# Local attention: exponentials that read the scores from PSUM with the negated row maximum as bias

## What is computed

```python
def local_attention(q, k, v):          # windows of 64, keys of this window and the one before
    sim = jnp.einsum('bhwid,bhwjd->bhwij', bq, bk)
    sim = jnp.where(mask, -jnp.finfo(sim.dtype).max, sim)
    attn = jax.nn.softmax(sim, axis=-1)
    return jnp.einsum('bhwij,bhwjd->bhwid', attn, bv)
...
q = l2norm(q) * qs; k = l2norm(k) * ksc
q, k = rotary_xpos(q, k)
o = local_attention(q, k, v)
x = x + o @ wo
# then shift_token, layernorm, h @ w1 + b1, a * gelu(g), h @ w2 + b2, added to x
```

## Time and profile before

| what | value |
|---|---|
| median of three runs | 1563.13 us |
| the profiled execution | 1563.58 us |
| its span | 1561.7 us |
| PE busy | 1346.8 us, 86% of the span |
| DVE busy | 1145.6 us, 73% |
| ACT busy | 801.7 us, 51% |
| POOL busy | 724.0 us, 46% |
| granted TensorE clock, mean | 0.947 |

### The profile page before, as it was taken

The page is one execution under the profiler, slowest core; times in us unless marked ns, Lnnn a source line. Parts: engine busy times, 40 slices in busy tenths (PEclk is TensorE's granted clock), DMA queues, the critical chain, the costliest instruction groups (busy, mean ns, idle before and its releaser), DMA issues.

```text
span 1561.7 us, 39029 instructions
## 1 busy us (share of the span) xinstructions
PE 1346.8 (86%) x15968; PEld 970.4 (62%) x15968; DVE 1145.6 (73%) x2484; ACT 801.7 (51%) x1633; POOL 724.0 (46%) x562
## 2 busy tenths in 40 slices
PE   4545999988999999984999999967989999998797
PEld 3434878875777777762666666654556666665554
DVE  3776776434888888874888888864578888888565
ACT  1222223224666666653777777742457777776421
POOL 1752545541344433434666666632246666666100
PEclk7776999996999999997999999999999999999999
DMA  4000544500000000003000100011100000000011
GB/s 133 0 0 16 112 93 110 108 13 2 3 3 3 4 3 3 3 3 91 8 8 7 22 8 8 1 30 28 25 24 8 9 17 13 9 5 2 12 31 54
DMA packets 61837, 40.34 MB, mean 26 GB/s; under 512 B 41312, under 2 KB 51808, under 8 KB 61664
## 3 DMA queue, kind: packets, MB, share of 16 engines
q1 hardware_dynamic: 61664, 37.88, 10.2%
HBM read 27.12 MB, written 2.36 MB: 19 GB/s over the span
## 4 chain that ended last, share of the span: by engine, by line
PE 33%; ACT 8%; SPq 6%; DVE 4%; POOL 2%; issue 1%; DMA 1%; DVEq 0%; POOLq 0%; ACTq 0%
PE PS L1872 7%; SPq L1463 5%; PE PS L1923 5%; PE PS L1957 4%; PE PS L1914 4%; PE PS L1891 3%; PE PS L1937 2%; ACT e_oT L1787 2%; PE PS L1948 2%; ACT qk L1756 2%; ACT e_pm L1793 2%; PE PS L1907 2%; POOL rot L1537 2%; PE PS L2010 1%; PE PS L2019 1%
## 5 line engine op out<-in xcount | busy, mean ns | idle before, releaser
L1537 POOL TENSOR_TENSOR rot<-qk,sinl 128x1024 f32<-128x1024 f32 x64 | 217.6, 3401 | 139.4 <-DVE qk L1631 139.4
L1530 POOL TENSOR_TENSOR rn<-ss,neghalf 128x16 f32<-128x16 f32 x64 | 185.6, 2901 | 108.6 <-DVE ss L1624 108.6
L1756 ACT ACTIVATE qk<-PS 128x512 f32<-128x512 f32 x128 | 76.4, 597 | 135.7 <-PE PS L1872 135.7
L1102 DVE TENSOR_REDUCE d_mx<-PS 128x4 f32<-128x576 f32 x128 | 96.9, 757 | 66.3 <-PE PS L1246 63.3
L1872 PE MATMUL PS<-wqkv,hT 128*128 128x512 f32 x256 | 128.8, 626 | 10.9 <-DMA qks<-in_e_ks 5.7
L607 POOL TENSOR_TENSOR uu<-uu,cb 128x512 f32<-128x512 f32 x64 | 82.8, 1295 | 90.0 <-DVE uu L839 88.2
L1923 PE MATMUL PS<-ident,e_pm 128*128 128x128 f32 x512 | 84.5, 289 | 45.9 <-ACT e_pm L1793 44.3
L1923 PEld LDWEIGHTS PS<-ident,e_pm 128*128 128x128 f32 x512 | 55.9, 144 | 102.4 <-ACT e_pm L1793 95.7
L739 ACT ACTIVATE sg<-PS 128x512 f32<-128x512 f32 x72 | 43.0, 597 | 134.1 <-PE PS L667 133.0
L1165 ACT ACTIVATE pa<-PS 128x512 f32<-128x512 f32 x128 | 76.5, 597 | 61.8 <-PE PS L1255 61.7
L1610 DVE TENSOR_REDUCE e_mx<-PS 128x8 f32<-128x1024 f32 x64 | 78.2, 1222 | 30.7 <-PE PS L1914 30.6
(11 more groups left out here) (241 smaller groups left out, 3535.9 us busy)
## 6 DMA issues: line engine op xcount, KB each, us to landing
cb<-comb_rows SPq DMA_DIRECT2D x32, 512.0 KB, 9.1
X<-in_L_attn_x SPq DMA_DIRECT2D x4, 512.0 KB, 7.4
zs<-Z SPq DMA_DIRECT2D x64, 32.0 KB
zg<-Z SPq DMA_DIRECT2D x16, 128.0 KB
out_x<-X SPq DMA_DIRECT2D x8, 256.0 KB, 2.5
zs<-Z SPq DMA_DIRECT2D x64, 31.8 KB
zg<-Z SPq DMA_DIRECT2D x16, 127.0 KB
wqkv<-in_e_wqkv SPq DMA_DIRECT2D x2, 768.0 KB, 4.2
```

The source lines that it names most:

```text
L1102: chain(dve.tensor_reduce(mx[:, par, :, :], s, AX.X, ALU.max))
L1530: pool.tensor_tensor(rn[:, v % 2, :], ss[:, v % 2, :], c.neghalf[:, :], ALU.pow).then_inc(rn_ready.sem, 1)
L1537: pool.tensor_tensor(rot[:, :, :, :], x, bc(sinl[:, t, :, :], 2, H2), ALU.mult).then_inc(rot_ready.sem, 1)
L1756: last = act.activation(qk[:, v % 4, s, :, :].rearrange("p h e -> p (h e)"), PS[:, QBANK + s, :], ACT.Copy)
```

## The change

`shift` becomes `maxima`: one reduction with the sign turned, into a tile `mx` with two slots, and no subtraction. `exponent` issues four activations of 128 x 128 instead of one of 128 x 512. Each reads one head's scores from PSUM and takes that head's negated maximum, one column of `mx`, as a per-partition bias. The second copy of `take_features` moves between `exponent(u,0)` and `exponent(u,1)`. The signal `qk_taken` is raised by each copy, and its waits count double. `scores` of the next unit and the first matmul of the feed-forward part wait for the exponentials instead of the subtractions.

```diff
-                def shift(L, v):
+                def maxima(L, v):
                     dve.wait_ge(s_ready.sem, s_ready.at(n(L, v)))
+                    if n(L, v) > 2:
+                        dve.wait_ge(p_exp.sem, p_exp.at(2 * (n(L, v) - 2)))
                     s = PS[:, SBANK:SBANK + 2, :].rearrange("p r (j k) -> p r j k", k=2 * W2)
-                    steps(dve.tensor_reduce(mx[:, :, :], s, AX.X, ALU.max))
-                    for h in range(2):
-                        if n(L, v) > 2:
-                            dve.wait_ge(pT_psum.sem, pT_psum.at(2 * (n(L, v) - 2) - 1 + h))
-                        dve.tensor_tensor(pm[:, v % 2, h, :, :, :], s[:, :, 2 * h:2 * h + 2, :],
-                                          bc(mx[:, :, 2 * h:2 * h + 2], 3, 2 * W2), ALU.subtract).then_inc(p_shifted.sem, 1)
+                    dve.tensor_reduce(mx[:, v % 2, :, :], s, AX.X, ALU.max, negate=True).then_inc(max_ready.sem, 1)
...
-                def take_features(L, v):
-                    for s in range(2):
-                        act.wait_ge(eqkv_ready.sem, eqkv_ready.at(2 * n(L, v) - 1 + s))
-                        last = act.activation(qk[:, v % 4, s, :, :].rearrange("p h e -> p (h e)"), PS[:, QBANK + s, :], ACT.Copy)
-                    last.then_inc(qk_taken.sem, 1)
+                def take_features(L, v, s):
+                    act.wait_ge(eqkv_ready.sem, eqkv_ready.at(2 * n(L, v) - 1 + s))
+                    act.activation(qk[:, v % 4, s, :, :].rearrange("p h e -> p (h e)"), PS[:, QBANK + s, :],
+                                   ACT.Copy).then_inc(qk_taken.sem, 1)
...
                 def exponent(L, v, h):
-                    act.wait_ge(p_shifted.sem, p_shifted.at(2 * n(L, v) - 1 + h))
-                    p = pm[:, v % 2, h, :, :, :].rearrange("p r j k -> p (r j k)")
-                    act.activation(p, p, ACT.Exp).then_inc(p_exp.sem, 1)
+                    if h == 0:
+                        act.wait_ge(max_ready.sem, max_ready.at(n(L, v)))
+                    if n(L, v) > 2:
+                        act.wait_ge(pT_psum.sem, pT_psum.at(2 * (n(L, v) - 2) - 1 + h))
+                    for r in range(2):
+                        for j in range(2):
+                            at = 2 * h + j
+                            last = act.activation(pm[:, v % 2, h, r, j, :], PS[:, SBANK + r, at * KEYS2:(at + 1) * KEYS2], ACT.Exp,
+                                                  bias=mx[:, v % 2, r, at:at + 1])
+                    last.then_inc(p_exp.sem, 1)
...
-                        take_features(L, u + 4)
+                        take_features(L, u + 4, 0)
                     if has(u):
                         exponent(L, u, 0)
+                    if has(u + 4):
+                        take_features(L, u + 4, 1)
+                    if has(u):
                         exponent(L, u, 1)
                         take_p(L, u, 0)
...
                     if v >= 1:
-                        pe.wait_ge(p_shifted.sem, p_shifted.at(2 * n(L, v - 1)))
+                        pe.wait_ge(p_exp.sem, p_exp.at(2 * n(L, v - 1)))
```

More of the change, by code:

```diff
@@ L1384, in local_transformer @@
         pa = ssb("e_pa", [P, 2, 4, P])
-        mx = ssb("e_mx", [P, 2, 4])
+        mx = ssb("e_mx", [P, 2, 2, 4])
         rz = ssb("e_rz", [P, 2, 4])
@@ L1403, in local_transformer @@
         qk_ready, qkT_psum, qkT_ready = signal("qk_ready"), signal("qkT_psum"), signal("qkT_ready")
-        s_ready, p_shifted, p_exp = signal("e_s_ready"), signal("e_p_shifted"), signal("e_p_exp")
+        s_ready, max_ready, p_exp = signal("e_s_ready"), signal("e_max_ready"), signal("e_p_exp")
         pT_psum, pT_ready, o_psum = signal("e_pT_psum"), signal("e_pT_ready"), signal("e_o_psum")
@@ L1626, in norm @@
                 def norm(L, v):
-                    dve.wait_ge(qk_taken.sem, qk_taken.at(n(L, v)))
+                    dve.wait_ge(qk_taken.sem, qk_taken.at(2 * n(L, v)))
                     dve.wait_ge(rn_ready.sem, rn_ready.at(n(L, v)))
@@ L1646, in attend @@
                     if has(u):
-                        shift(L, u)
+                        maxima(L, u)
                     if u == nunits - 3:
@@ L1751, in features @@
                     act.activation(h_of(v), PS[:, QBANK, 0:P], ACT.Copy).then_inc(eh_ready.sem, 1)
-                def take_features(L, v):
-                    for s in range(2):
-                        act.wait_ge(eqkv_ready.sem, eqkv_ready.at(2 * n(L, v) - 1 + s))
-                        last = act.activation(qk[:, v % 4, s, :, :].rearrange("p h e -> p (h e)"), PS[:, QBANK + s, :], ACT.Copy)
-                    last.then_inc(qk_taken.sem, 1)
+                def take_features(L, v, s):
+                    act.wait_ge(eqkv_ready.sem, eqkv_ready.at(2 * n(L, v) - 1 + s))
+                    act.activation(qk[:, v % 4, s, :, :].rearrange("p h e -> p (h e)"), PS[:, QBANK + s, :],
+                                   ACT.Copy).then_inc(qk_taken.sem, 1)
                 def squares(L, v):
-                    act.wait_ge(qk_taken.sem, qk_taken.at(n(L, v)))
+                    act.wait_ge(qk_taken.sem, qk_taken.at(2 * n(L, v)))
                     if n(L, v) > 1:
@@ L1859, in turn_z @@
                     elif has(v - 1):
-                        pe.wait_ge(qk_taken.sem, qk_taken.at(n(L, v - 1)))
+                        pe.wait_ge(qk_taken.sem, qk_taken.at(2 * n(L, v - 1)))
                     elif L:
@@ L1887, in turn_qk @@
                     if has(v + 3):
-                        pe.wait_ge(qk_taken.sem, qk_taken.at(n(L, v + 3)))
+                        pe.wait_ge(qk_taken.sem, qk_taken.at(2 * n(L, v + 3)))
                     for s in range(2):
@@ L2002, in up @@
                         pe.wait_ge(w_loaded.sem, w_loaded.at(16 * 5 * (L + 1)))
-                        pe.wait_ge(p_shifted.sem, p_shifted.at(2 * n(L, nunits - 1)))
+                        pe.wait_ge(p_exp.sem, p_exp.at(2 * n(L, nunits - 1)))
                     elif g == 0 and j == 1:
```

## The result

The changed kernel takes 1575.9 us (median of four, 1574.71 to 1578.94), against 1562.23 us for the kernel before in the same comparison: a ratio of 1.0085, with a 95% interval from 1.0062 to 1.0108. That is 10 to 17 us more. The forecast was 1583 us, 20 us more; the range of 1570 to 1600 holds the time. The profiled execution took 1578.94 us with a span of 1577.1 us, 15.4 us over the profiled execution before.

The account below looks back on a forecast made before the run. PE bounds the kernel but waits on ACT's `take_p(0)` before `turn_p(1)`. 56 regular steps at 0.36 us later make 20.2 us, other terms 0: from the 1563.13 median to 1583 us, range 1570 to 1600.

Parts of the forecast that it names:

- DVE's relief: On DVE, two subtractions fewer, 1.20 us a step; off the path, so 0 in the sum.
- One sign: On DVE and POOL, normalisation, `by_sine` and `rotated` can move up by some 0.7 us, giving PE nothing.
- The price of an exponential: On ACT, 128 columns with a bias pointer: step 0.265 us, duration 0.37; eight make 2.12 us against about 1.03 for two old.
- `take_p(0)` was to be 0.36 us late: ACT's line reaches `take_p(0)` at 912.62 against 912.26; `turn_p(1)` on PE moves 0.36 us later, the step becomes 10.21 us.
- The moved waits: Waits of `scores`, the `mx` and `pm` slots and `turn_qk` on exponentials or copies: claimed to cost nothing.
- The steps without `project_qk`: Steps 28 to 31 of each layer, without q and k copy: set at 0, within 0.3 us each.
- point 1's bound for DVE: DVE's relief bounded by 0 below and, if wrong about what releases the scores, DVE's whole 1.20 us as a gain.
- Rival A: On ACT, the pointer costs more per 128 columns: step 0.29 to 0.36 us, time 1594 to 1626; 14%.
- rival B: On ACT, pointer fetch hides, step 0.1625 us; PE gets back 0.35 us a step, time 1543; 10%.
- rival C: Effects cancel: exponential's step near 0.22, or `turn_p(1)` tied to `turn_qk` with slack swallowing 0.36 us; 1563; 8%.
- the half on `turn_qk`: Rival C's case on PE: `turn_p(1)` tied to `turn_qk`, not `take_p(0)`, with slack to swallow the 0.36 us.
- the step near 0.22: Rival C's other case, on ACT: an exponential's step near 0.22 us, where faster turns to slower; time 1563.

Follow-up runs that it names:

- the kernel whose step was 0.16 us: The changed kernel with no bias pointer on its eight exponentials and the maximum's subtraction left out of the softmax: 1533.4 us, ratio 0.9783.
- the experiment on it: The kernel before with four instead of eight transposes in `turn_qk`, half of q and k left out of the attention: 1565.77 us, ratio 1.0007.

## Why the prediction was right

1. DVE's relief is worth nothing in a regular step: right. What it frees turns into idle time before the maxima: 1.36 us in a regular step, against 0.53 in the kernel before. One sign was off: `by_sine` was to come 0.7 us earlier relative to the maxima and comes 1.3 earlier (915.22 - 912.78 = 2.44 us behind them, against 912.28 - 908.52 = 3.76). The working had kept POOL's `powers` in its place; in the changed kernel it starts 2.06 us ahead of the maxima instead of 1.19. It costs nothing.

2. The exponentials start 0.50 us behind the q copy (forecast 0.48): right.

3. The price of an exponential, the term on which the sum hung. Forecast: a step of 0.265 us, a duration of 0.37. Measured: 0.25 and 0.394. The queue's completion is nearer to the forecast than the starts: from the q copy to the end of `take_p(0)` it is 3.65 us, and less three copies (0.48, 0.48, 0.60) 0.26 remain for each of the eight. From the figures of the Trainium skill, page "ScalarE: Activation LUTs", section "What ACT_TABLE_LOAD costs", the prediction estimated a duration of 387 ns, and the trace agrees (394). The step of 294 ns estimated from the same section does not come true, since neighbours overlap by 0.14 us here and not by 0.093.

4. `take_p(0)` was to be 0.36 us late and `turn_p(1)` with it. `take_p(0)` is 0.26 us late (2.98 - 2.72), but is itself longer, 0.67 instead of 0.60 us, and `turn_p(1)` follows at 0.81 instead of 0.75 us: 0.32 us. Mechanism and place right, the size 0.04 too large: 56 x 0.04 = 2 us of the sum. That it is so near is partly luck: the queue up to `take_p(0)` was forecast 0.10 us too long, and the 0.06 us by which `turn_p(1)` follows it later were not in the forecast.

5. The moved waits cost nothing: right. The exponentials end at 916.96, and PE begins the next mask matmuls at 921.25 with no idle time.

6. The steps without `project_qk` were set at 0 within 0.3 us each. This was wrong: the one from unit 28 to 29 gained 1.15 us in each layer. The step that failed counted ACT's and PE's rows there but not that DVE, with the statistics in its queue, had no slack; point 1's bound for DVE should have been applied here. The last one, from unit 30 to 31, missed the other way in layer 0: it grew from 10.58 to 11.59 us (in layer 1 from 10.78 to 11.05). The rows of this stretch in layer 0, before and changed (window, length, busy time of PE, PEld, DVE, ACT and POOL, granted clock, DMA) show PE at a lower clock. A granted clock of 1.00 is the level of 2.4 GHz, one of 0.5 that of 1.2 GHz, and both stretches mix the two:

```profile
1038.50:1049.00 10.50, 7.81 (x95) 6.67 (x96) 3.96 (x9) 4.00 (x7) 1.21 (x2) 0.84 0.03 5
...
1045.00:1056.50 11.50, 9.12 (x95) 7.64 (x96) 2.66 (x7) 4.95 (x13) 1.21 (x2) 0.70 0.02 4
```

PE had idled about 3 us before `turn_p(0)` in both (3.26 and 3.03 us). Why the mean granted clock is 0.84 in one and 0.70 in the other was not tried.

The starts of the maxima add up to the 15.4 us of the span. The units up to 28 of both layers give 17.7 (forecast 20.2). The last three steps of each layer take back 0.3 and 1.0. Unit 0 started 1.0 us earlier in that execution, ahead of anything that the change touches. What lies between and behind the layers comes to 0.03.

Rival A (a dearer pointer, a step of 0.29 or more) and rival B (a free one, 0.16) are both refuted by the step of 0.25 us, which falls to 0.16 only when the pointer is gone. Rival B's time was worked out with the end of `project_v` as a bound for `turn_p(0)`, which it is not; the kernel whose step was 0.16 us ran in 1533 us and not in 1543. Of rival C, the half on `turn_qk` is refuted by the experiment on it, and the step near 0.22 by the measured one.

## What to carry to other kernels

Before moving an operation to an engine that is half idle, find the last instruction on that engine that another engine waits for, and add up what now stands in front of it; the busy share (51% here) says nothing about it. A per-partition bias costs nothing per column and 0.09 us per instruction here: the step with a pointer is 0.25 us for 128 columns, 0.36 for 256 and 0.57 for 512, and it grows by the column as fast as the steps without one (0.16 and 0.48). So share the bias over as many columns as the arithmetic allows, or leave the subtraction where it is. A change in several parts may hide a gain and a loss: here the move alone gave 0.7%, and the eight exponentials took it back and more. Nor do the parts simply add: the same move gave 0.24, 0.37 or 0.64 us a step, by what stood around it.

## What was not expected of the hardware

A copy behind a train of short activations takes longer in the records though its own work is the same: `take_p(0)` 0.60 us behind two of 512 columns, 0.64 behind 256, 0.67 behind 128 with a pointer and 0.71 behind 128 without. So for short activations the distance of starts (0.16 us without a pointer) understates what reaches the next engine. The cause of the lag was not tried. And a matmul group can follow one that is recorded to run 0.16 us longer (910.92 + 1.02 against 911.78). The kernel before had such a pair too: `turn_qk` at 912.06, `turn_p(0)` recorded until 911.57 + 0.65.
